# Transposing x by matmuls with the identity in 64x64 tiles, next to the gram of the chunk before

## What is computed

```python
inner = x[:, ROW, :] * x[:, COL, :]                  # (2048, 780, 64)
h = jax.nn.relu(jnp.einsum('bpe,he->bph', inner, W1) + b1)
logits = jnp.einsum('bph,oh->bpo', h, W2) + b2
attn = jax.nn.softmax(logits, axis=1)
pooled = jnp.sum(inner * attn, axis=1)
y = pooled @ Wl.T + bl                               # (2048, 1)
```

## Time and profile before

| | us |
|---|---|
| median of 3 runs | 1154.47 |
| lowest and highest | 1153.91, 1154.53 |
| profiled execution, device time | 1153.29 |
| its span in the profile | 1151.4 |
| PE busy | 1128.6 (98%) |
| DVE busy | 1056.9 (92%) |
| ACT busy | 982.9 (85%) |

### The profile page before, as it was taken

How to read it: one execution, slowest core, us unless ns; L and a number is a source line. 1 busy time by engine, 2 the same in 40 slices (tenths; PEclk the granted TensorE clock), 3 DMA queues, 4 the chain that set the end, 5 groups by cost and what they waited for, 6 DMA issues and landing times.

```text
span 1151.4 us, 63299 instructions
## 1 busy us (share of the span) xinstructions
PE 1128.6 (98%) x29001; PEld 534.3 (46%) x29001; DVE 1056.9 (92%) x1691; ACT 982.9 (85%) x1219; POOL 0.7 (0%) x6
## 2 busy tenths in 40 slices
PE   6999999999999999999999999999999999999995
PEld 3444444444444444444444444444444444444442
DVE  7999999899999989999899998999999999998983
ACT  5888888888888888888888888888888888888884
POOL 0000000000000000000000000000000000000000
PEclk9999999999999999999999999999999999999997
DMA  2221221222121121211312212121122213113010
GB/s 58 42 66 32 61 39 29 62 40 55 36 60 35 37 64 29 66 29 34 69 28 63 40 26 66 35 59 37 30 63 39 57 34 68 30 35 69 14 43 2
DMA packets 220376, 51.31 MB, mean 45 GB/s; under 512 B 216016, under 2 KB 216016, under 8 KB 220112
## 3 DMA queue, kind: packets, MB, share of 16 engines
q1 hardware_dynamic: 220112, 47.27, 20.0%
HBM read 34.11 MB, written 13.12 MB: 41 GB/s over the span
## 4 chain that ended last, share of the span: by engine, by line
PE 98%; DVE 1%; SPq 1%; ACT 0%; DMA 0%; issue 0%; ACTq 0%
PE slot L296 60%; PE logit_bank L316 29%; PE slot L277 4%; PE slot L264 4%; DMA x_rows<-in_r_x 0%; PE slot L342 0%; SPq L193 0%; ACT hidden L369 0%; DVE weighted L468 0%; SPq L223 0%; SPq L227 0%; SPq L225 0%; SPq L230 0%; DVE logits L448 0%; DVE row_max L452 0%
## 5 line engine op out<-in xcount | busy, mean ns | idle before, releaser
L369 ACT ACTIVATE hidden<-slot,b_col 128x780 f32<-128x780 f32 x1024 | 875.9, 909 | 115.9 <-PE slot L296 115.8
L431 DVE TENSOR_TENSOR inner<-xt 128x760 f32<-128x760 f32 x1024 | 909.5, 943 | 58.8 <-PE slot L296 58.1
L296 PE MATMUL slot<-inner,w_block 64*32 64x390 f32 x16384 | 782.8, 490 | 0.0
L296 PEld LDWEIGHTS slot<-inner,w_block 64*32 64x32 f32 x16384 | 300.7, 107 | 326.4 <-issue 281.5
L316 PE MATMUL logit_bank<-hidden,w_window 64*32 64x390 f32 x8192 | 442.1, 487 | 0.6 <-ACT hidden L369 0.6
L316 PEld LDWEIGHTS logit_bank<-hidden,w_window 64*32 64x32 f32 x8192 | 152.8, 105 | 186.4 <-ACT hidden L369 81.5
L277 PEld LDWEIGHTS slot<-xt,x_scaled 64*40 64x40 f32 x4096 | 45.4, 117 | 40.6 <-issue 40.6
L353 ACT COPY xt<-slot 128x640 f32<-128x640 f32 x64 | 44.4, 694 | 19.6 <-PE slot L264 19.6
L361 ACT COPY gram_rows<-slot 128x640 f32<-128x640 f32 x64 | 44.4, 694 | 18.3 <-PE slot L277 18.3
L438 DVE TENSOR_TENSOR inner<-xt 128x80 f32<-128x80 f32 x256 | 59.5, 233 | 0.0
L264 PE MATMUL slot<-ident,x_rows 128*128 128x128 f32 x320 | 50.1, 288 | 9.3 <-DMA x_rows<-in_r_x 9.3
(11 more groups left out here) (28 smaller groups left out, 27.2 us busy)
## 6 DMA issues: line engine op xcount, KB each, us to landing
x_rows<-in_r_x SPq DMA_DIRECT2D x128, 160.0 KB, 3.0
gram<-gram_dram SPq DMA_DIRECT2D x32, 400.0 KB, 3.7
gram_dram<-gram_rows SPq DMA_DIRECT2D x512, 12.5 KB
gram_dram<-gram_rows SPq DMA_DIRECT2D x256, 25.0 KB
w_rows<-in_L_rec_W SPq DMA_DIRECT2D x2, 16.0 KB, 2.3
wl_col<-in_L_rec_Wl SPq DMA_DIRECT2D x2, 0.2 KB, 2.3
b_col<-in_L_rec_b SPq DMA_DIRECT2D x2, 0.2 KB, 2.3
w_window<-in_L_rec_W SPq DMA_DIRECT2D x2, 0.2 KB, 2.3
```

Of the source, the lines that this page charges most:

```text
L296: last = nc.tensor.matmul(banks[to:to + QUAD, ab * BANK:ab * BANK + HALF], w1_block[rows, of:of + QUAD], inner[rows, at:at + HALF], start= ...
L369: nc.scalar.activation(hidden[s % RING][:, half * PAIRS:(half + 1) * PAIRS].rearrange("p (a n) -> p a n", a=2), banks_of("layer", s, half) ...
L431: nc.vector.tensor_tensor(window_view(inner, to + half * HALF, [[PAIRS, STEP_DUOS], [SPAN, SHIFTS], [1, SPAN]]), window_view(fields, at + ...
```

## The change

The transposes of a chunk become 20 matmuls with the identity as the moving operand. Each takes 64 rows of `x_rows` (`r`) and one half of the batch (`half`) as 64 stationary columns, in the tile of the array at row 64 r and column 64 half. The two values of r go to the two banks of the slot, as the gram's `ab` does, so ACT's copy reads the slot in another pattern, with the same 640 elements for each partition. The constants become -13 and -5: the turn of chunk n and the gram of chunk n - 1 now fall behind the same step, 8n - 13, and the turn is put first, on PE, on ACT and in the table of places.

```diff
--- before.py
+++ after.py
@@ -150,8 +150,8 @@
             return 5 * (s // 2 + 1)
 
 
-        TURN_AT = -12
-        GRAM_AT = -7
+        TURN_AT = -13
+        GRAM_AT = -5
         SPREAD_AT = -3
 
         gram_after = {max(n * CHUNK_STEPS + GRAM_AT, 1 + n): n for n in range(CHUNKS)}
@@ -163,10 +163,10 @@
         for s in range(STEPS):
             place["layer", s, 0] = len(place)
             place["layer", s, 1] = len(place)
+            if s in turn_after:
+                place["turn", turn_after[s]] = len(place)
             if s in gram_after:
                 place["gram", gram_after[s]] = len(place)
-            if s in turn_after:
-                place["turn", turn_after[s]] = len(place)
 
         def count_to(*what):
 
@@ -261,8 +261,14 @@
                 pe.wait_ge(x_loaded[n % 2], 32 * (n // 2 + 1))
                 wait_for_slot("turn", n)
                 for t in range(TT):
-                    last = nc.tensor.transpose(banks_of("turn", n)[:, t * P:(t + 1) * P],
-                                               x_rows[n % 2][:, t, :, :].rearrange("p h e -> p (h e)"), ident[:, :])
+                    for r in range(2):
+                        rows = slice(r * TILE, (r + 1) * TILE)
+                        at = r * BANK + t * TILE
+                        for half in range(2):
+                            last = nc.tensor.matmul(
+                                banks_of("turn", n)[half * TILE:(half + 1) * TILE, at:at + TILE],
+                                x_rows[n % 2][rows, t, half, :], ident[rows, rows], start=True, stop=True,
+                                tile_position=(r * TILE, half * TILE))
                 last.then_inc(slots_filled, 1)
 
             def gram_matrix(n):
@@ -330,10 +336,10 @@
                 first_layer(s, 1)
                 if s:
                     score(s - 1)
+                if s in turn_after:
+                    turn_chunk(turn_after[s])
                 if s in gram_after:
                     gram_matrix(gram_after[s])
-                if s in turn_after:
-                    turn_chunk(turn_after[s])
             score(STEPS - 1)
 
             pe.wait_ge(stats_kept, ROUNDS)
@@ -350,9 +356,10 @@
 
                     act.wait_ge(inner_ready, inner_to((n - XT_RING + 1) * CHUNK_STEPS - 1))
                     act.wait_ge(slots_filled, count_to("gram", n - XT_RING))
-                nc.scalar.copy(window_view(xt[n % XT_RING], 0, [[EXT, CHUNK_DUOS], [TT, U], [1, TT]]),
-                               window_view(banks_of("turn", n), 0, [[U, CHUNK_DUOS], [1, U], [P, TT]])).then_inc(
-                                   slots_emptied, 1)
+                nc.scalar.copy(window_view(xt[n % XT_RING], 0, [[CHUNK_DUOS // 2 * EXT, 2], [EXT, CHUNK_DUOS // 2],
+                                                                [TT, U], [1, TT]]),
+                               window_view(banks_of("turn", n), 0, [[BANK, 2], [U, CHUNK_DUOS // 2], [1, U],
+                                                                    [TILE, TT]])).then_inc(slots_emptied, 1)
 
             def copy_gram(n):
                 act.wait_ge(slots_filled, count_to("gram", n))
@@ -386,10 +393,10 @@
             for s in range(STEPS):
                 relu(s, 0)
                 relu(s, 1)
+                if s in turn_after:
+                    copy_turned(turn_after[s])
                 if s in gram_after:
                     copy_gram(gram_after[s])
-                if s in turn_after:
-                    copy_turned(turn_after[s])
                 for j in range(STEP_DUOS):
                     r, after = (s - EXP_AT[j]) // ROUND_STEPS, (s - EXP_AT[j]) % ROUND_STEPS
                     if r > 0 and after == 0:
```

## The result

| us | before | changed |
|---|---|---|
| median (20 runs each) | 1154.06 | 1151.24 |
| lowest and highest | 1152.71, 1155.47 | 1147.81, 1154.71 |
| profiled execution | 1153.29 | 1151.28 |
| its span | 1151.4 | 1149.4 |

The ratio is 0.9975, with an interval of 0.9968 to 0.9983: 2.8 us faster, where 15.8 were forecast, and outside the range of 1134 to 1146. The runs of the changed kernel also spread over 6.9 us, those of before over 2.8.

What follows compares the result with a forecast made beforehand. PE was taken to bound the kernel (98% of the chain that ended last). Pairs -16.7, ACT in a round's first chunk +0.8 and the head +0.1 sum to -15.8 us: 1154.47 to 1138.7 us, range 1134 to 1146.

Steps and rivals of the forecast that it cites:

- Twenty matmuls 64x64 come: PE's new matmuls in the loop: 40 MATMULs, ten rounds of four tiles at 0.058 us, costing 0.58 us a chunk.
- Size of the pair: New matmuls with the gram on PE: 0.58 - 0.85 = -0.27 us net, times 62 = -16.7 us.
- Entry and exit: On PE, changing tile shape costs about 0.25 us a visit; the new matmuls take over the gram's entry, nothing new paid.
- Rival A: Within a round, column neighbours don't overlap: 0.116 instead of 0.058 us a round, 1174.7 us; chance 0.07.
- Rival B: Between new matmuls and gram a shape change still costs 0.25 us, leaving -0.02 us a pair, 1154 us; chance 0.06.
- Rival C: ACT's copy takes back 0.1 us a pair at the slot, 6.2 us in all, 1144.9 us; chance 0.07.
- ACT in a round's first chunk: With two exponentials besides, one slot or score load is late by 0.05 to 0.1 us; fifteen rounds, +0.8 us.
- DVE: DVE multiplies ahead of PE; the new pace takes about 1.1 us of each round's spare time, more than half left.
- The head: Chunks 0 and 1 turn ahead of the loop, each part costing 0.06 us more than five transposes: +0.1 us.
- What would show it wrong: In the changed profile: DVE's waits for PE vanish and PE waits for products; plain steps waiting for ACT mean Rival C.

## Why the prediction was wrong

- **The step that failed** is "Twenty matmuls 64x64 come", which costed them by their streaming alone. They are also 80 instructions in place of ten, directly ahead of the gram's 128. The supply of these instructions was not a term of the sum: it costs 11 to 12 us in the profiled execution. With it the loop gets shorter by 14.5 (61 x 0.24, undisturbed) less 11.3, that is 3.2 us; the head, 0.65 us later, takes part of that back, and the spans differ by 2.0. With the supply mostly mended the kernel takes 1140.2 us, 1.5 from the forecast of 1138.7 and 13.7 under the kernel before of the same series (1153.91), of 15.8 forecast.
- **Size of the pair.** -0.27 us was forecast, -0.24 came in undisturbed chunks. The new matmuls take 0.63 us to the gram, not 0.58, outside the ends of 0.55 to 0.61. The 0.058 us a round was right; the slow first round of 0.107, as the gram has one, was not counted.
- **Entry and exit.** Right in size and mostly in mechanism. The prediction took 0.25 us a visit and had one visit less. Standing together saves 0.16 us a pair with the old transposes (17.51 to 17.35) and 0.28 with the new matmuls (17.55 to 17.27). The prediction did not say that the larger part comes with unlike shapes too. Both fit a price of 0.12 to 0.16 us for each change of shape, an estimate from these four chunks; the rule that the prediction cited from the Trainium skill (TensorEngine Tiling (Array Packing), Key Properties), that changing the tiling mode drains TensorE, agrees with that count.
- **Rival A** (neighbours on one row half don't overlap): no, 0.63 us in either order. **Rival B** (the pair changes shape): no gap between the two groups. **Rival C** (ACT gives it back): the copies take 0.69 us as forecast. Its sign, weight loads that wait for ACT, did come: 54 times for the copy, 9.4 us in all and 0.2 at the most. But no MATMUL waited with them, and the step after an undisturbed pair takes its 1.99 us.
- **ACT in a round's first chunk**, +0.8 us: not seen; the windows give 17.31 us for the one with the exponentials (23 instructions on ACT), 0.04 over the next, and in the kernel before such chunks are 0.03 over the others as well. **DVE**: its waits for PE are still 57.9 us in 79 times, against 58.1 in 92 of the earlier trace rows, so it keeps ahead. **The head**: the first layer starts at 12.69, before at 12.04, but the matmuls ahead of it also start later, at 11.42 instead of 10.78, when x lands. From there to the layer it is 1.27 us against 1.26, so the new turn costs nothing there.
- What would show it wrong was named as plain steps that wait for ACT, or PE waiting for products. What came, a stop with no releaser, was not on the list.

What stays open: why a pair is harmless 95 instructions into a block and not 205. Either way the pair lies across a border, between a block of about 3.0 us and one of 4.5. When exactly a fetch is asked for, the trace doesn't say, and no run tests it. Nor is it shown which of the two loads, the grams' or x's, holds the fetch up.

## What to carry to other kernels

Many small matmuls on PE have a second price besides their streaming: each fp32 one here is four instructions (two MATMULs and two weight loads), and a dense run of them can outpace the fetch of code. Count instructions per us around such a run. Where q8's packets land shortly before a stop with no releaser, or groups grow busier while their MATMULs stay as long, move the run or spread it, keep large loads away from it, and only then judge the matmuls themselves.

## What the hardware showed besides

- Instruction blocks of 256 reach PE only about one block ahead, at least 3.3 us apart, and are used no sooner than 1.2 us after they land; the longest standstill of PE was 1.40 us. The cost is not "mostly hidden", as the Trainium skill (Runtime: NRT & Kernel Launch, Instruction fetch mechanics) has it, for code this dense: 1144.0 against 1163.7 us with equal instructions.
- Large loads can hold up the fetch: with 0.80 MB in 2.4 us on the DMA engines (96.5% busy) no instruction block came until their end, and moving the loads took 1143.97 us to 1140.17. In other rounds a block came in the midst of such a load.
- Tiles of PE can run out of step by 0.15 us for several steps (groups of 1.67 us instead of 1.52, steps still 1.97) and pay at a later change of shape, 0.17 us in the stretch shown.
- Fp32 matmuls of 64x64x64 in four tiles cost 0.63 us for twenty beside the gram, 0.74 us beside scores and layer in 64x32 tiles, in either order of row and column halves beside the gram.
